# Attention, expert mixture and refinement in one kernel: a finer first hand-over, a merged gate and softplus product, block 1's first layer ahead of block 0's units, and the last two blocks finished on VectorE

## What is computed

```
x = x + layernorm(attention(layernorm(x)))       # latent q and kv, rope, clip at 80, causal softmax
z = layernorm(x); v = 0                          # router picks 2 of 8 experts per token from z
twice:
    ctrl = gelu([z, v] @ w1 + b1) @ w2 + b2      # for the shared and the 2 chosen experts: a, b, g
    v'   = sigmoid(a) * v - softplus(b) * (z - mu)
    z'   = z + 0.1 * sigmoid(g) * v'             # then mixed over the 3 slots and with a halting share
x = x + layernorm(z0 + iw * (gelu(z @ wf1) @ wf2))   # "refine"
```

## Time and profile before

| what | us |
|---|---|
| median of 3 runs | 2655.97 |
| the profiled execution itself | 2656.04 |
| its span (first to last instruction) | 2654.3 |
| outside the span | 1.7 |
| PE busy | 2462.7 (93%) |
| DVE busy | 2246.4 (85%) |
| ACT busy | 1888.9 (71%) |
| POOL busy | 635.3 (24%) |
| mean granted clock of PE | 0.962 |

### The profile page before, as it was taken

The page is one execution under the profiler, slowest core; times in us unless marked ns, Lnnn a source line. Parts: engine busy times, 40 slices in busy tenths (PEclk is TensorE's granted clock), DMA queues, the critical chain, the costliest instruction groups (busy, mean ns, idle before and its releaser), DMA issues. The chain is left out here.

```text
span 2654.3 us, 42371 instructions
## 1 busy us (share of the span) xinstructions
PE 2462.7 (93%) x15736; PEld 1751.5 (66%) x15736; DVE 2246.4 (85%) x3849; ACT 1888.9 (71%) x3011; POOL 635.3 (24%) x427
## 2 busy tenths in 40 slices
PE   5999999999999976999999999999999999999997
PEld 2333334333333335888888888888888888888997
DVE  5788887887887786989999999999999999977555
ACT  2787787878778845676767676766776777765886
POOL 2113221221322202112121211212121212110676
PEclk8999999999999977999999999999999999999999
DMA  6462644626264511000000000000010000003332
GB/s 134 76 100 85 104 90 80 110 73 100 84 104 76 124 41 43 10 26 10 17 26 26 11 17 26 26 10 19 24 26 11 21 21 18 18 1 102 117 120 80
DMA packets 149631, 146.50 MB, mean 55 GB/s; under 512 B 19922, under 2 KB 131794, under 8 KB 149428
## 3 DMA queue, kind: packets, MB, share of 16 engines
q1 hardware_dynamic: 149428, 143.80, 24.2%
HBM read 97.22 MB, written 46.53 MB: 54 GB/s over the span
## 5 line engine op out<-in xcount | busy, mean ns | idle before, releaser
L577 ACT ACTIVATE probs<-psum_a 128x1024 f32<-128x1024 f32 (+3 forms) x768 | 600.3, 815 | 201.7 <-PE psum_a L950 198.6
L1678 PE MATMUL psum_f<-w,picked 128*128 128x256 f32 (+1 forms) x2304 | 717.2, 344 | 0.0
L1677 PE MATMUL psum_f<-w,picked 128*128 128x256 f32 x2304 | 622.9, 287 | 12.2 <-DVE picked L1489 10.3
L1678 PEld LDWEIGHTS psum_f<-w,picked 128*128 128x128 f32 x2304 | 444.2, 193 | 51.4
L1677 PEld LDWEIGHTS psum_f<-w,picked 128*128 128x128 f32 x2304 | 444.2, 193 | 16.5 <-issue 11.9
L950 PE MATMUL psum_a<-q_stack,k_stack 72*128 72x512 f16 (+3 forms) x1536 | 380.7, 338 | 23.9 <-ACT probs L577 16.8
L660 DVE TENSOR_SCALAR probs<-probs 128x2048 f32<-128x2048 f32 (+3 forms) x320 | 320.1, 1000 | 83.0 <-ACT probs L577 82.8
L1489 DVE TENSOR_TENSOR picked<-hid,masks 128x512 fp32r<-128x512 f32 x512 | 369.7, 782 | 7.2 <-PE psum_f L1678 3.8
L1322 ACT ACTIVATE gates<-psum_f 128x256 f32<-128x256 f32 (+1 forms) x384 | 185.1, 487 | 249.8 <-PE psum_f L1678 208.6
L965 PE MATMUL psum_a<-probs,v 128*17 128x512 f32 (+3 forms) x3072 | 337.3, 512 | 11.8 <-DVE probs L660 5.0
L950 PEld LDWEIGHTS psum_a<-q_stack,k_stack 72*128 72x128 f16 x1536 | 98.9, 99 | 358.4 <-ACT probs L577 208.9
(11 more groups left out here) (299 smaller groups left out, 5168.5 us busy)
## 6 DMA issues: line engine op xcount, KB each, us to landing
heads_scratch<-kq_parts SPq DMA_DIRECT2D x64, 256.0 KB
k_stack<-heads_scratch SPq DMA_DIRECT2D x84, 128.0 KB
q_stack<-heads_scratch SPq DMA_DIRECT2D x84, 128.0 KB
x_in<-x_dram SPq DMA_DIRECT2D x8, 1024.0 KB, 5.5
x_res<-x_dram SPq DMA_DIRECT2D x16, 512.0 KB, 5.8
xs<-x_scratch SPq DMA_DIRECT2D x16, 512.0 KB, 3.9
xf_scratch<-xs SPq DMA_DIRECT2D x16, 512.0 KB, 2.9
xf<-xf_scratch SPq DMA_DIRECT2D x16, 512.0 KB, 6.2
```

Source lines behind the costliest of these rows:

```text
L577: act.activation(probs[:, s % PROB_SETS, 2 * u:2 * u + 2, q0:512], psum[:, 2 * u:2 * u + 2, q0:512], ACT.Exp, scale=exp_scale).then_inc(ex ...
L1677: pe.matmul(soft_out, x, cols[:, 1], start=start, stop=stop)
L1678: return pe.matmul(gate_out, x, cols[:, 2] if it == 0 else cols[:, 0::2], start=start, stop=stop)
```

## The change

1. Attention: the second semaphore is split. Groups 1 and 2 to 3 are loaded by separate calls of `stack` with a semaphore each, and `scores` waits for that of its group. 12 more DMAs for each half, the same bytes.
2. Mixture, round 0: `both` makes one product of 512 columns (`w[:, D:3 * D]`, b and g side by side) into bank `AG_BANK + s` in place of two of 256. ACT's softplus reads its part from that bank. Round 1 is as before.
3. Mixture, order at the start: for block 0 LG comes ahead of EDGE, and MT behind H2. All of block 1's first layer but MT runs ahead of unit 0; MT stays behind unit 1.
4. POOL at the start of the mixture: `x_scale(1)` first, then it waits for the choice of block 0 (`onehot_ready`), then come block 0's and block 1's low parts.
5. Refine: DVE takes the row statistics of each half directly behind its add. The last two blocks leave the chain of DVE shift, ACT scale and POOL add; DVE finishes them itself (`finish`: four `tensor_scalar`, one `tensor_tensor`) behind all else, with a semaphore of their own for the store.

```diff
                 stack(0, 0, 1, cols, first_stacked[half][0])
-                stack(0, 1, GROUPS - 1, cols, first_stacked[half][1])
+                stack(0, 1, 1, cols, first_stacked[half][1])
+                stack(0, 2, GROUPS - 2, cols, first_stacked[half][2])
...
                 if u == 0 and j == 0 and b == 0:
-                    pe.wait_ge(first_stacked[c][min(g, 1)], 16 * STACK_DMAS)
+                    pe.wait_ge(first_stacked[c][min(g, 2)], 16 * STACK_DMAS)
...
     def first_layer(k):
+        if k == 0:
+            return [[("RT", k, 0, 0), ("H", k, 0, SHARED), ("LG", k, 0, 0), ("H", k, 0, EDGE)],
+                    [("H", k, 0, 0), ("H", k, 0, 1), ("H", k, 0, 2)], [("MT", k, 0, 0)]]
...
         if kind == "first":
+            if gi == 0:
+
+                rows, h, _ = first_layer(k)
+                return [first_x(k) + rows + h[0:2] + [("H", k, 0, 2)], [], [("MT", k, 0, 0)], []]
...
             pool.wait_ge(weights_ready, 1)
+            x_scale(1)
+
+            pool.wait_ge(onehot_ready, 1)
             for m in (EDGE, *range(FULL)):
                 lower_parts(("H", 0, 0, m))
-            x_scale(1)
+            for job in fills(0)[0]:
+                if job in gel_turn:
+                    lower_parts(job)
...
-                src = soft_psum[:, slots.start * D:slots.stop * D]
-                act.activation(soft_b[:, n % 2, slots], src.rearrange("p (s n) -> p s n", n=D), ACT.Softplus).then_inc(b_read, 1)
+                if unit_of(n)[1] == 0:
+                    src = psum[:, AG_BANK + slots.start:AG_BANK + slots.stop, 0:D]
+                else:
+                    src = soft_psum[:, slots.start * D:slots.stop * D].rearrange("p (s n) -> p s n", n=D)
+                act.activation(soft_b[:, n % 2, slots], src, ACT.Softplus).then_inc(b_read, 1)
...
+                    if it == 0:
+                        return pe.matmul(gate_out, x, w[:, D:3 * D], start=start, stop=stop)
                     cols = w.rearrange("p (c n) -> p c n", n=D)
                     pe.matmul(soft_out, x, cols[:, 1], start=start, stop=stop)
-                    return pe.matmul(gate_out, x, cols[:, 2] if it == 0 else cols[:, 0::2], start=start, stop=stop)
+                    return pe.matmul(gate_out.rearrange("p (c n) -> p c n", n=D), x, cols[:, 0::2], start=start, stop=stop)
...
-                if k >= 3:
+                if 3 <= k < BLOCKS - DVE_LAST + 3:
                     pool.wait_ge(scaled, k - 2)
...
-                if k >= 2:
+                if 2 <= k < BLOCKS - DVE_LAST + 2:
                     scale(k - 2)
...
-                dve.wait_ge(dve_read, dve_value[("RF", k, 1)])
-                for t in range(BT):
-                    last = dve.bn_stats(stats[:, t, :], y[:, k % BUFS, t, :])
+                    dve.wait_ge(dve_read, dve_value[job])
+                    for t in (2 * i, 2 * i + 1):
+                        last = dve.bn_stats(stats[:, t, :], y[:, k % BUFS, t, :])
...
+            def finish(k):
+
+
+                dve.wait_ge(rstd_ready, k + 1)
+                rows = y[:, k % BUFS]
+                for t in range(BT):
+                    last = dve.tensor_scalar(rows[:, t, :], rows[:, t, :], y_mean[:, k % 2, t:t + 1], y_rstd[:, k % 2, t:t + 1],
+                                             ALU.subtract, ALU.mult)
+                then_wait(last)
+                dve.tensor_tensor(rows, rows, x1[:, k % BUFS], ALU.add).then_inc(y_last_ready, 1)
...
+            for k in range(BLOCKS - DVE_LAST, BLOCKS):
+                finish(k)
```

More of the change, by code:

```diff
@@ L308, in attention @@
         stacked = [sem(f"stacked{g}") for g in range(GROUPS)]
-        first_stacked = [[sem(f"first_stacked{half}{i}") for i in range(2)] for half in range(2)]
+        first_stacked = [[sem(f"first_stacked{half}{i}") for i in range(3)] for half in range(2)]
         scores_ready = sem("scores_ready")
@@ L355, in write_scratch @@
                 if b == 2:
-                    for i in range(2):
+                    for i in range(3):
                         sp.wait_ge(first_stacked[0][i], 16 * STACK_DMAS)
@@ L1668, in second_layer @@
                 soft_out = soft_psum[:, D * s:D * s + D]
[L1669 to L1672, removed]
+                gate_out = psum[:, AG_BANK + s, :]
                 def both(x, w, start=False, stop=False):
+                    if it == 0:
+                        return pe.matmul(gate_out, x, w[:, D:3 * D], start=start, stop=stop)
                     cols = w.rearrange("p (c n) -> p c n", n=D)
                     pe.matmul(soft_out, x, cols[:, 1], start=start, stop=stop)
-                    return pe.matmul(gate_out, x, cols[:, 2] if it == 0 else cols[:, 0::2], start=start, stop=stop)
+                    return pe.matmul(gate_out.rearrange("p (c n) -> p c n", n=D), x, cols[:, 0::2], start=start, stop=stop)
                 if n > 0:
@@ L1786, in refine @@
         y_ready = sem("r_y_ready")
+        y_last_ready = sem("r_y_last_ready")
+        DVE_LAST = 2
         def bank(job):
@@ L1822, in _ @@
             for k in range(BLOCKS - 3, BLOCKS):
-                sp.wait_ge(y_ready, k + 1)
+                if k < BLOCKS - DVE_LAST:
+                    sp.wait_ge(y_ready, k + 1)
+                else:
+                    sp.wait_ge(y_last_ready, k - (BLOCKS - DVE_LAST) + 1)
                 sp.dma_start(out_v[k], y[:, k % BUFS]).then_inc(stored[k % BUFS], 16)
@@ L1938, in y_shifts @@
                                          op0=ALU.mult, op1=ALU.mult).then_inc(shift_ready, 1)
-            for k in range(-1, BLOCKS + 2):
+            def finish(k):
[6 more added lines that the diff above has]
+                dve.tensor_tensor(rows, rows, x1[:, k % BUFS], ALU.add).then_inc(y_last_ready, 1)
+            for k in range(-1, BLOCKS + 1):
                 if k + 1 < BLOCKS:
@@ L1944, in _ @@
                     add_bias(k)
-                if k >= 2:
+                if 2 <= k < BLOCKS:
                     y_shifts(k - 2)
```

## The result

The changed kernel takes 2645.84 us (median of 5 runs, 2644.31 to 2648.42), the kernel before, run beside it, 2656.37 (2653.72 to 2660.41). The ratio is 0.9957, with a 95% interval of 0.9946 to 0.9968: 11 us faster. Forecast were 2643.5, between 2635 and 2651.

A forecast was written before the change was run, and what follows sets the result against it. Neither PE nor DVE was called the bound from shares; DVE was taken to close the mixture's periods. 2656.04 - 6.0 (start) - 2 (seam) - 4.4 (tail) - 0 (periods) = 2643.6, rounded 2643.5 us, range 2635 to 2651.

The forecast's parts named there:

- Start: Start of attention: PE's 3.87 us DMA wait goes and full clock behind it saves 2.1 us; together 6.0.
- The rival that the split does nothing: Start of attention: group 1's stack lands no earlier because DMA rings are full; no gain there, 2649.6 us; chance 0.07.
- (a): Seam into the mixture: with LG ahead of EDGE, DVE's route for block 0 starts 2.1 us sooner.
- (b): Seam: POOL waits for block 0's choice, saving 2.9 us; choice 5 us sooner, `mask_columns(0)` ends 3.5 us earlier.
- (c): Seam: with `x_scale(1)` first, `x_normalize(1)` no longer waits 5.16 us for POOL; ends at 1022.6, at worst 1026.
- (d): Seam: block 1's layer ahead of unit 0 makes unit 0's integration 1.7 to 4.4 us later, taken as 2.5.
- (e): Seam, DVE's chain to the pick: POOL's five block-1 steps drop out, 4.7 us, and waiting for LG, 1.4.
- (f): Seam: PE newly idles some 6 us for block 1's choice, then starts slowly, costing 1.7 us.
- only the idle goes: Rival: clock at the start stays low (3.9 us gained) and the seam costs 1.5; 2649.2 us, chance 0.17.
- Periods: Mixture's repeating periods: merged product saves PE 7.5 us, but DVE closes each period, so 0 is gained.
- Slower, by the clock: Rival: PE's longer pick waits before round-1 groups each bring a clock fall, 14 x 1.55 = 21.7 us; 2665, chance 0.06.
- Tail: End of refine: finishing on DVE saves 2.6 us, earlier statistics 1.3, block 14's shift 0.6; 4.4 after 0.1 back.

The follow-up runs named there:

- part 1 alone: Only the split of the first stacks' load and semaphore, on the kernel before: 2650.68 us beside 2657.43, ratio 0.9976.
- the pair of kernels above: Changed kernel with block 1's first layer again behind units 0 and 1, 2641.47 us; changed kernel with the old order of block 0's jobs too, 2638.34 us.
- part 2 alone: Only the merged product of 512 columns in round 0, on the kernel before: 2653.59 us, ratio 0.9986.
- the relieved kernels: Changed kernel with one of DVE's two slot adds left out in round 0: 2628.98 us with two products, 2615.45 us with the merged one.

## Why the prediction was right or wrong

**Right, by parts that were off in both directions.** 2643.5 was predicted and 2645.8 measured; the mechanisms of start, periods and tail held, that of the seam did not. That the total came so near is in part that the seam was the smallest of the three sums that had a gain in them.

**Start.** Forecast 6.0 (3.9 to 7.6), measured 6.2 over the profiles and 6.8 in the time of part 1 alone. The forecast read the wait of 3.87 us from a single profile; that this one lay near the mean of 1.13 to 5.64 was luck. Wait and slow clock went together, and the 12 added DMAs cost nothing that shows. The rival that the split does nothing is out.

**Seam.** Forecast -2 (-5 to +2), measured +0.2. Step by step, counted from the entry:
- (a) LG ahead of EDGE: the route starts 1.8 us sooner (12.3 for 14.1), forecast 2.1. Right, and worth next to nothing: with MT in its old place it runs at 17.9 us after the entry whether LG is ahead or not.
- (b) The level steps at 0.42: right, the choice comes 5.6 sooner. `mask_columns(0)` follows by 2.4, not 3.5, because MT waits behind the H jobs. This is the first step that failed. I had put MT's move down as "gain less"; in the pair of kernels above, with MT in its old place, `pick(0)` is 1.5 us earlier although the choice is later (17.9 for 16.1).
- (c) `x_normalize(1)` doesn't wait for POOL, but three of its four `tensor_scalar` are held up: 4.07 for 1.38 us. Counted from the entry it ends 4.9 sooner (26.5 for 31.4), forecast 5.2 to 8.6.
- (d) The mis-sized term. `integrate(0)` starts 5.4 us later, forecast 1.7 to 4.4 (from the forecast's own times, 1047.5 to 1050, it is 4.2) and taken 2.5. From unit 0's first product to `integrate(0)` it took 8.1 us, as forecast (8 to 8.9). The miss is ahead of that: unit 0 starts 10.2 us later, forecast 5.6 to 9. The 2.5 stood for POOL holding up little; it held up three operations, and `x_normalize(1)` ended 0.3 us behind the late end of (c). From there to unit 0 it is 16.8 us where the forecast has 16.
- (e) From there DVE comes to round 1 in 36.2 in place of 41.3 us, 5.2 less, with a new wait of 1.41 for the gates of unit 2 in it: 6.6, forecast 6.1. Right.
- (f) The wait of 5.85 for some 6, and 1.4 for 1.7. Right as a cost; but I took it as given. The runs show that it was the seam's lever: with the choice made where DVE idles it is gone, and 5.4 us with it.

The sum of the measured terms is 5.4 - 6.6 + 1.4 = 0.2. What I had not asked is what each part brings alone: POOL's order brings 6.1 us, and the moves beside it take them. For the seam the rival "only the idle goes" (+1.5, because of (f)) came nearer than the forecast, but its start was wrong.

**Periods.** Forecast 0 of 7.5 us. Measured 0.06 a period, 0.7 us in the twelve between the first and the last pick wait. That is for the periods alone; the time of part 2 alone, 3.8 us less (1.3 to 6.1), says that the merged product is worth more than the 0 taken for it, 1.3 us of it in the seam and the rest not located. That DVE closes a period was right, and the relieved kernels show it from the other side. The pick wait was forecast at 1.1 and is 0.94: a merged pair saves 0.37 / 96 = 0.0039 us, not 0.0049. The distance of starts on the two sides came from different kinds of work, and the difference of two nearly equal distances carries that error. The price of the Trainium skill, "TensorE: Matmul & The Clock Gate", section "Back-to-back issue gap" (2.5 ns a product, which the section gives for a product on its own), is off the other way, by 1.4 ns a pair where the forecast was off by 1.0.

**Slower, by the clock.** No fall came behind a pick wait of 0.94: that rival is out as it was put. (It counted 14 such waits; the trace before has 13.) In the relieved kernels the pick wait is gone and most falls behind the LG wait are gone too. The forecast had the clock only as a possible loss behind the pick, and not as a possible gain elsewhere.

**Tail.** Forecast 4.4 (3.4 to 4.8), measured 4.8 in every profile with part 5. From the last product to the variance 2.4 in place of 4.4 us, 1.95 (forecast 1.9); from there to the last add 5.1 in place of 7.95, 2.85 (2.6); the store's way is unchanged (3.5 us), so nothing was given back.

**The sum.** In the profiled execution 12.4 us were forecast and 10.3 came. The seam is 2.2 short and the start 0.6; the tail gave 0.4 more and refine 0.3. Between round 1 and refine both stand at 1356.3: the merged product's gain there, some 1.5 us, and one fall of the clock more than before, near 2353 us, cancel.

## What to carry to other kernels

An edit of several parts is costed part by part and alone: here the order on POOL gained 6 us, and the reordering beside it gave all of it back. When a step is brought forward, follow it to the transfer that someone waits for: a choice that was ready 5.6 us sooner brought the masks only 2.4 us sooner, since the transpose behind it stood in the queue. A wait for a transfer that is read from one profile can be another in the next (1.13 to 5.64 us here); several profiles of the unchanged code say what it is worth. And a saving on an engine that only waits longer for another one is kept in store: it pays when that other one is relieved, as 0.37 us a period did here.

## What the runs showed of the hardware

POOL's subtraction of 128 x 512 holds up DVE's `tensor_scalar` with a single SBUF input too. The line of `x_normalize(1)` in the kernel after (ns min/median/max):

```profile
L1424 DVE TENSOR_SCALAR xs<-xs,row_scale x4: 400/1264/1380, 1015.6 to 1019.3; 128x256 f32<-128x256 f32 x4
```

and POOL beside it, and below that POOL beside `finish(14)`:

```profile
1015.32 3.88 POOL L1258 TENSOR_TENSOR hid<-gel,hid 128x512 fp32r<-128x512 f32 x3
...
2635.43 1.25 POOL L1861 TENSOR_TENSOR y_rstd_r<-y_veps_r,half_neg_r 128x4 f32<-128x4 f32 x1 [2.31 <-DVE y_veps_r L1952]
```

The forecast had assumed such holds but only had rows for two inputs. It is in line with the Trainium skill, "GPSIMD Engine Reference", section "1. Specifications", which names 2-port modes beside two inputs; whether this operation runs in such a mode no run here shows. In `finish` the same operation ran beside POOL's power of 128 x 4 at its full speed, four in 1.38 us; there it was POOL that took 1.25 in place of 1.02 us.

A relief of 0.71 us for DVE in each of 64 units made the kernel with the merged product 30.4 us faster (2615.45 beside 2645.84). Of that 15.3 us are 13 periods of 85.28 in place of 86.46, and 10.9 are seven falls of the clock fewer, 1.55 each; 4.2 lie outside the periods. Every fall in the periods comes behind PE's wait for LG, but that wait does not decide it: it is 1.41 to 1.43 us each time, and in the kernel after 8 of 13 periods have a fall and 5 have none (clock 0.98 and 1.00 over the period). With the add left out two things changed at once: the pick wait of 0.6 to 0.9 us, behind which no fall ever came, is gone, and the period is shorter (85.3 for 86.5 us), so that the LG waits follow one another at another distance. Which of the two takes the falls away is not separated here, and there is one profile of each relieved kernel.
